# A two-layer image model on one core: layer 0 on a 98x97 grid, and the residual of the output placed by PE transposes

## The reference

```python
x = x + _L0_conv_ref(_gn(x), ...)   # layer 0
x = x + _L1_conv_ref(_gn(x), ...)   # layer 1
```

## Time and profile before

| | |
|---|---|
| median of 3 runs | 6339.48 us (6336.2 to 6344.21) |
| profiled execution, first to last instruction | 6343.7 us |
| PE busy | 6036.5 us (95%) |
| DVE busy | 5685.5 us (90%) |
| ACT, POOL busy | 5097.3 us (80%), 5209.8 us (82%) |
| first product of the recurrence (L1134) starts | 328.2 us |
| mean granted TensorE clock | 0.965 |

### The profile page before, as it was taken

How to read it: one execution, slowest core, us unless ns; L and a number is a source line. 1 busy time by engine, 2 the same in 40 slices (tenths; PEclk the granted TensorE clock), 3 DMA queues, 4 the chain that set the end, 5 groups by cost and what they waited for, 6 DMA issues and landing times. The chain is left out here.

```text
span 6343.7 us, 99100 instructions
## 1 busy us (share of the span) xinstructions
PE 6036.5 (95%) x32260; PEld 3123.0 (49%) x32260; DVE 5685.5 (90%) x4459; ACT 5097.3 (80%) x8658; POOL 5209.8 (82%) x5092
## 2 busy tenths in 40 slices
PE   8999999999999999999999999999999999998776
PEld 5645445454554545545455544545455454554222
DVE  0089999999999999999999999999999999999998
ACT  4588888888888888888888788888888888887664
POOL 0078888888888888888888888888888888888988
PEclk9999999999999999999999999999999999998665
DMA  3367676676767667675676767667676766767553
GB/s 95 88 165 170 160 167 157 163 162 169 169 154 168 155 165 170 155 182 142 167 162 162 173 156 169 155 164 163 167 169 156 166 154 165 168 142 160 129 124 75
DMA packets 805826, 983.25 MB, mean 155 GB/s; under 512 B 391258, under 2 KB 417542, under 8 KB 805318
## 3 DMA queue, kind: packets, MB, share of 16 engines
q1 hardware_dynamic: 805318, 976.92, 65.4%
HBM read 717.71 MB, written 259.00 MB: 154 GB/s over the span
## 5 line engine op out<-in xcount | busy, mean ns | idle before, releaser
L1181 POOL TENSOR_TENSOR hc<-hs,cs 128x512 f32<-128x512 f32 x3072 | 3835.6, 1271 | 692.7 <-DVE hs L1140 505.6
L1140 DVE TENSOR_TENSOR_SCAN hs<-av,state,b 128x512 f32<-128x512 f32 x2688 | 3257.8, 1263 | 88.6 <-POOL state L1185 4.9
L1008 ACT ACTIVATE av<-rep_d,nega 128x512 f32<-128x512 f32 x3072 | 2096.7, 713 | 41.5 <-DVE hs L1140 36.8
L1134 DVE TENSOR_TENSOR b<-rep_u,pb 128x1536 f32<-128x1536 f32 x1024 | 1803.5, 1761 | 211.0 <-PE pb L846 124.7
L855 PE MATMUL py<-hc,rsel 128*32 128x512 f32 x6144 | 1141.6, 634 | 40.6 <-POOL hc L1181 39.7
L769 PE MATMUL cb<-xu,w1a 96*128 96x392 f32 x2400 | 984.3, 513 | 27.7 <-DVE b1a L1120 17.4
L774 PEld LDWEIGHTS cb<-w2c,g 128*98 128x98 f32 x9600 | 885.9, 167 | 169.7 <-issue 106.9
L774 PE MATMUL cb<-w2c,g 128*98 128x96 f32 x9600 | 910.7, 252 | 17.4 <-ACT g L956 9.3
L956 ACT ACTIVATE g<-cb,b1a 128x392 f32<-128x392 f32 x1200 | 679.5, 579 | 87.0 <-PE cb L769 78.8
L810 PE MATMUL cb<-xn,wtap 96*96 96x512 f32 x1536 | 723.3, 607 | 2.4 <-ACT xn L1029 2.4
L769 PEld LDWEIGHTS cb<-xu,w1a 96*128 96x128 f32 x2400 | 414.5, 191 | 415.4 <-issue 199.3
(11 more groups left out here) (109 smaller groups left out, 6703.4 us busy)
## 6 DMA issues: line engine op xcount, KB each, us to landing
rep_d<-delta_scratch SPq DMA_DIRECT2D x512, 384.0 KB, 7.0
rep_u<-deltax_scratch SPq DMA_DIRECT2D x512, 384.0 KB, 6.3
cs<-c_scratch SPq DMA_DIRECT2D x512, 256.0 KB, 5.9
delta_scratch<-dlt SPq DMA_DIRECT2D x128, 384.0 KB, 3.1
deltax_scratch<-dlt SPq DMA_DIRECT2D x128, 384.0 KB, 9.2
t1r<-t_scratch SPq DMA_DIRECT2D x160, 240.0 KB, 6.5
v_scratch<-v2s SPq DMA_DIRECT2D x192, 192.0 KB
xb<-in_x SPq DMA_DIRECT2D x128, 192.0 KB, 4.6
```

The lines of the kernel that those rows point to most:

```text
L1008: act.activation(av[:, n % NAV, :], rep_d[:, k % 2, j, :], ACT.Exp, scale=nega[:, q, j:j + 1])\
L1134: dve.tensor_tensor(b3[:, :, :], rep_u[:, k % 2, 3 * hf:3 * hf + 3, :], pb[:, None, :].broadcast_to([128, 3, T]), ALU.mult).then_inc(dve_b ...
L1140: dve.tensor_tensor_scan(hs[:, n % NHS, :], av[:, n % NAV, :], b3[:, n % 3, :], start, ALU.mult, ALU.add)\
L1181: pool.tensor_tensor(hc[:, n % NHC, :], hs[:, n % NHS, :], cs[:, k % 2, g % NQ, :], ALU.mult)\
```

## The change

The grid constants become 98 and 97. There are still 25 blocks, but the last has two columns, not four: its `W_up` is one product, its `W_f` 194 columns, its `W_2` 6 products and its `W_dn` 192 columns. In `out` the residual comes first, as a transpose of x1, and the two products accumulate on it. The planner's cost for OUT goes from 2.70 to 2.25 us, and with it the slots of some W steps.

```diff
-GW, GH = 100, 98
-NB = GW // 4
+GW, GH = 98, 97
+NB = (GW + 3) // 4
 BC = 4 * GH
...
+def wide(b):
+
+    return min(4, GW - 4 * b)
...
 PE_US = {"ST": 0.45, "SA": 0.70, "SB": 0.70, "W_up": 0.70, "W_f": 0.71, "W_2": 2.10, "W_dn": 0.75, "D_lo": 1.20, "D_hi": 1.20,
-         "X": 2.72, "Z": 0.92, "DBC": 1.82, "DT": 0.50, "OUT": 2.70, "WARM": 0.215}
+         "X": 2.72, "Z": 0.92, "DBC": 1.82, "DT": 0.50, "OUT": 2.25, "WARM": 0.215}
...
                 elif name == "W_up":
-                    for e in range(2):
+                    for e in range(wide(b) // 2):
...
-                    mm = pe.matmul(bank[:, 0:BC], w1a[:, 128 * f:128 * f + 128], xu[:, b % 2, :],
+                    n = wide(b) * GH
+                    mm = pe.matmul(bank[:, 0:n], w1a[:, 128 * f:128 * f + 128], xu[:, b % 2, 0:n],
                                    start=True, stop=True)
                 elif name == "W_2":
-                    for j in range(4):
+                    for j in range(wide(b)):
...
-                        mm = pe.matmul(bank[half, 0:4 * C], dn_h[:, :], vr[:, e % 2, :], start=True, stop=True)
+                        n = wide(e) * C
+                        mm = pe.matmul(bank[half, 0:n], dn_h[:, :], vr[:, e % 2, 0:n], start=True, stop=True)
...
                     o = bank[:, C * b:C * b + C]
+                    pe.transpose(o, x1o[:, tb], ident[0:C, 0:C])
                     for t in range(2):
-                        pe.matmul(o, xcs[:, p, t, tb], wo[:, t, :], start=(t == 0), stop=False)
-                    mm = pe.matmul(o, x1o[:, tb], ident[0:C, 0:C], start=False, stop=True)
+                        mm = pe.matmul(o, xcs[:, p, t, tb], wo[:, t, :], start=False, stop=(t == 1), skip_group_check=True)
```

More of the change, by code:

```diff
@@ L510, in load_t1 @@
             def load_t1(w, m):
+                n = min(5, GW // 2 - 5 * m)
                 src = t1_d[bass.ds(w, 1)].rearrange("o w f -> (o w f)").rearrange(
-                    "(i p c) -> p i c", p=128, c=C)[:, 5 * m:5 * m + 5, :]
-                sp.dma_start(t1r[:, m % 2], src).then_inc(t1_ld[m % 2], 16)
+                    "(i p c) -> p i c", p=128, c=C)[:, 5 * m:5 * m + n, :]
+                sp.dma_start(t1r[:, m % 2, 0:n], src).then_inc(t1_ld[m % 2], 16)
             def load_rr(d, m):
@@ L573, in step @@
                     sp.sem_inc(sp_passed, 1)
-                    rows = HH * min(2, NB - 2 * b)
-                    dst = v2_d[x, :, 8 * b:8 * b + rows // 16, :].rearrange("h (e w) c -> e h (w c)", w=4)
-                    sp.dma_start(dst, v2s[0:rows, b % 2]).then_inc(v2_st[b % 2], 16)
+                    two, w = min(2, NB - 2 * b), wide(2 * b)
+                    dst = v2_d[x, :, 8 * b:8 * b + two * w, :].rearrange("h (e w) c -> e h (w c)", w=w)
+                    sp.dma_start(dst, v2s[0:HH * two, b % 2, 0:w * C]).then_inc(v2_st[b % 2], 16)
                 if name == "ST":
@@ L935, in step @@
                 elif name == "W_up":
-                    out, src = xu[:, b % 2, :], bank[0:C, 0:BC]
+                    n = wide(b) * GH
+                    out, src = xu[:, b % 2, 0:n], bank[0:C, 0:n]
                 elif name == "W_2":
-                    out, src = vr[:, b % 2, :], bank[0:GH, 0:4 * C]
+                    n = wide(b) * C
+                    out, src = vr[:, b % 2, 0:n], bank[0:GH, 0:n]
                 elif name == "W_dn":
                     act.wait_ge(v2_st[b % 2], count(v2_st[b % 2], x * (16 * (7 - b % 2)) + (b // 2) * 16))
-                    rows = HH * min(2, NB - 2 * b)
-                    out, src = v2s[0:rows, b % 2, :], bank[0:rows, 0:4 * C]
+                    rows, n = HH * min(2, NB - 2 * b), wide(2 * b) * C
+                    out, src = v2s[0:rows, b % 2, 0:n], bank[0:rows, 0:n]
                 elif name == "ST":
@@ L955, in step @@
                         act.wait_ge(cb_free[w % RING], st.freed(w))
-                    act.activation(g2[:, b % 2, f, :], bank[:, 0:BC], ACT.Square, bias=b1a[:, f:f + 1]).then_inc(fr, 1)
+                    n = wide(b) * GH
+                    act.activation(g2[:, b % 2, f, 0:n], bank[:, 0:n], ACT.Square, bias=b1a[:, f:f + 1]).then_inc(fr, 1)
                 elif name in ("D_lo", "D_hi"):
```

## The result

The changed kernel is slower: median 6373.31 us (four runs, 6369.82 to 6377.77) against 6337.84 us for the kernel before (four runs beside them), a ratio of 1.0054 [1.004, 1.0068]. The forecast was 6322.5 us, with 6296 to 6343 as its range.

A forecast was written before the change was run, and what follows sets the result against it. DVE's chain sets the pace except where PE delivers pb late; before the loop PE bounds. Thirteen full samples -6.5, before loop -4.3, sample 0 -4.8, sample 14 -0.5, last OUT -0.9: -17 us, from median 6339.5 to 6322.5 us, range 6296 to 6343.

The forecast's parts named there:

- slot 20: Where OUT(0) follows W_f(16,1) and waits for W_f(16,0)'s bank: net +1.9 us a full sample, bounds 0 and 2.5.
- Slot 139: W_2(3) moved ahead of the reduction, around OUT(4) and OUT(5): net 0 us a full sample, bounds -1.0 and +0.5.
- sample 0: Sample 0: -3 us from the PAD moved ahead of W_f(16,2) and W_2(15), -1.8 from later stalls, together -4.8 us.
- The transposes: Residual in each OUT by transpose, 20 instructions for 24: 0.45 us shorter per OUT, 3.6 us of PE a sample.
- The rival that transposes don't keep the clock up: Every OUT runs at 0.22 us an instruction, at a low granted clock, +1.5 us each: 6437 us, chance 2%.
- OUT(2): Slot 69, stalls around OUT(2) and the last W blocks: net -1.1 us a full sample, bounds -1.7 and -0.6.
- Behind OUT(6): Nothing moves there and the stall of 0.69 us goes: -0.6 us a full sample, bounds -0.6 and -0.2.
- at the PADs: Sample's end, where DVE waits for the PADs: -0.7 of 1.4 us a full sample, bounds -0.2 and -0.9.
- Before the loop: Stage bound by PE: W of sample 0 saves 3.9 us, plus half of sample 1's 0.4, together -4.3 us.
- Sample 14: The sample after the thirteen full ones: -0.5 us.
- the bank waits weigh more, slower: Rival: at three places PE is held by softplus's evacuations and ACT doesn't come forward; +2.0 us a sample, 6355, chance 10%.
- The re-sorting is free: Rival: ACT's eviction comes forward or the late pb is caught up; -4.3 us a sample, 6273 us, chance 16%.

The follow-up runs named there:

- the waits filled: Changed kernel with WARM products that compute nothing put into PE's waits in full samples, nine ahead of OUT(0), six ahead of W_2(3): 6317.12 us, 0.9955 of the kernel before.
- The swapped run: Changed kernel with OUT(0) again ahead of W_f(16,1) in the full samples, other moved steps kept: 6309.62 us, 0.995 of the kernel before.

## Why the prediction was wrong

**The step that failed** is slot 20's "Net +1.9 us", with "bounds 0 if ACT comes forward, 2.5 if there is no slack". Its mechanism was right: the bank of W_f(16,0), ACT's `g` as the releaser, an idle time of "over 2 us" (2.13), and, with the waits filled, +1.9 us in groups 7 and 8. The price was not. The steps behind the wait were costed at full clock: OUT(0) at 20 x 0.1115 = 2.23 us, and nothing for `pb`, W_f and W_2(15). At half clock OUT(0) to `pb` took 3.10 us in sample 4 (2.98 to 4.11 in the 13) and W_2(15) 3.71, so the stall grew to 3.31 us and a second of 1.71 us came behind it: in the mean +5.0 in groups 7 and 8, -0.5 in groups 9 to 19, +4.4 net, outside the bounds. Slot 139's "Net 0" failed in the same way: +0.5 with the wait filled, which is the bound that was given, and +1.6 as it ran. The two terms missed by 2.5 + 1.6 = 4.1 us a sample, 53 us over thirteen. The span came out 45.6 us above the sum (6372.3 against 6326.7); the other terms together gave 8 us back, though sample 0 gave less than forecast.

The prediction had the warning before it. It named a granted clock under 1.00 as what would prove it wrong (over samples 2 to 13 it is 0.98), but priced a fall of the clock for the transposes alone, and took the full clock of sample 6 as a fact of the kernel. PE's longest idle time in that stretch is 1.33 us. The trace of the kernel before also has one idle time of the forecast's size, 9 us behind that stretch, where an ST waits for its input, and the clock is at half behind it:

```profile
2799.74 0.93 PE L769 MATMUL cb<-xu,w1a 96*128 96x392 f32 x2 [1.33 <-DVE b1a L1120]
...
2976.84 1.01 PE L737 MATMUL cb<-ident,xb 128*96 128x128 f32 x4 [2.22 <-DMA xb<-in_x]
...
2976.90:2980.30 3.40, 3.40 (x11) 2.66 (x12) 2.16 (x3) 1.69 (x3) 3.14 (x4) 0.50 1.05 301
```

A forecast that adds an idle time of 2 us to PE has to price what PE does behind it.

**Point by point.**
- The transposes: right. An OUT came to 2.12 us, a transposed step to 0.09 us, and each stall behind OUT(5) to OUT(7) shrank by over 0.5 us. That ST's row is the right price, not the longer one, is borne out.
- The rival that transposes don't keep the clock up (2%): wrong. By the Trainium skill (TensorE: Matmul & The Clock Gate, Part 4: PE-mode transpose) a transpose isn't counted as other matmuls are; here the clock fell alike with identity products, in 13 of 13 samples, and with transposes in the old order it held there in 13 of 13. Whether a transpose counts for the clock was not measured.
- OUT(2): forecast -1.1, measured -1.3. The wait at the next bank's release was foreseen; that it could also take the clock down was not, and the transposes alone show that (in the kernel after it fell there in sample 2).
- Behind OUT(6) -0.6 and at the PADs -0.8: right.
- Before the loop: forecast -4.3, measured -7.1. PE is busy 5.5 us less there (289.9 to 284.4 us); the rest are shorter waits. Sample 0: -4.8 and -3.5. That their sum is right to 1.5 us is luck. Of the -3 at sample 0's first PADs only -0.9 came (groups 7 to 9); -1.9 that was not forecast came in groups 0 to 3, and +2.0 in groups 41 to 49, where the clock falls behind W_2(3) as in the full samples. The swapped run, whose order in sample 0 is that of the changed kernel, got -7.1 and -0.2: its granted clock from 321 to 345 us is 0.57, that of the kernel after 0.72. So sample 0's part isn't settled by these runs. Sample 14 gave -1.4 for -0.5, the last OUT's sample -1.1 for -0.9.
- The rival nearest to what happened is "the bank waits weigh more, slower" (10%): its places are right and its sign too, but its price (at most +2.0 us a sample, 6355) had no clock in it.
- "The re-sorting is free" (16%) describes what the change would have been worth in the old order: 6273 forecast, 6284 and 6274 measured without the re-sorting.

What stays open: why the clock fell behind W_2(3) in 10 of 13 samples and not in three, with the same wait of 1.37 us, and why the idle time of 1.33 us for `b1a`, shown above, is followed by a fall in only two of 13 samples, in the kernel before (samples 9 and 13) and in the kernel after (7 and 8). The length of a wait doesn't settle it. No run here tells what does.

## What to carry to other kernels

When a step moves in an in-order queue with a ring of buffers, work out whose release it now waits for, and then price two things: the wait, and the speed of the work behind it. A wait of PE can cost more in the granted clock than in itself: here 3.1 us of clock against 1.9 us of wait. Where a wait can't be moved, products that compute nothing, put into it, bought 56 us; a planner that is given a truer cost of one step should be made to keep the order that the banks allow, or it gives the saving back.

## What the runs showed of the hardware

- The clock falls on a PE that is busy 94% of the span. A single wait of 2.13 us was followed by the half clock in 13 of 13 samples, one of 1.37 us in 10 of 13, and two of 0.52 and 0.34 us (with one step of 0.9 us between them, in the run with the transposes alone) in 5 of 13. Another of 1.33 us in the kernels before and after was followed by it in 2 of 13.
- When the clock falls differs from sample to sample, though the wait of 2.13 us is the same. In sample 4 the first products of OUT(0) still run at full speed (0.61 us) and those from 1.2 us on at half (1.06). In sample 6 the first are slow already (from 2644.60 to 2645.60 us, with PE still waiting, the granted clock is 0.72), and groups 7 and 8 cost +6.8 us there against +4.8 in sample 4:

```profile
2645.61 0.42 PE L844 MATMUL cb<-ident,x1o 96*128 96x96 f32 x1 [2.14 <-ACT g L967]
2645.82 1.06 PE L846 MATMUL cb<-wo,xcs 96*128 96x96 f32 x4
```

- The fall then lasts: in sample 4 the granted clock is 0.50 from 1887.3 to 1891.0 and 0.61 over the next 4 us, though PE is busy throughout. The kernel after:

```profile
1887.30:1891.00 3.70, 3.70 (x16) 2.93 (x15) 1.03 (x1) 1.70 (x4) 3.62 (x4) 0.50 0.49 135
1891.00:1895.00 4.00, 4.00 (x28) 3.67 (x29) 3.91 (x4) 1.08 (x3) 1.19 (x1) 0.61 0.80 196
1895.00:1900.00 5.00, 5.00 (x27) 2.28 (x21) 3.20 (x3) 5.00 (x10) 3.88 (x4) 1.00 0.40 112
```

- Over many samples the mean hides this: over samples 2 to 13 the granted clock is 0.98 in the kernel after and 1.00 in the kernel before. Two hundredths of clock, placed where DVE waits for PE, turn a gain into a loss: with the waits filled, the same order is 25 us faster than the kernel before.
